# Attention and gated FFN on one core: norm roots in a PSUM bank, bias adds in the up stage, the even output's transposes in slot 15, scores for the maxima as pairs of 64-row tiles

## What is computed

```python
def attn(q, k, v, Wq, Wk, Wv, Wfc, bfc):          # q normalised, k = v = context
    score = einsum('bhqd,bhkd->bhqk', qh, kh) / sqrt(16)   # 32 heads of 16, K and V repeated 4 times
    out = einsum('bhqk,bhkd->bhqd', softmax(score), vh)
    return merge(out) @ Wfc.T + bfc
def ffn(x, w_gating, w_linear):                   # operands cast to fp8, results bf16
    return qdot(gelu(qdot(x, w_gating[0])) * qdot(x, w_gating[1]), w_linear)
x = x + attn(layernorm(x), ctx, ctx, ...)
x = x + ffn(layernorm(x), ...)
```

## Time and profile before

| | us |
|---|---|
| median of 3 runs | 466.82 |
| lowest and highest | 464.19, 467.55 |
| span of the profiled execution | 470.4 |
| busy: TensorE | 429.2 (91%) |
| busy: VectorE | 340.6 (72%) |
| busy: ScalarE | 314.8 (67%) |
| busy: GpSimd | 237.4 (50%) |
| `up` matmuls L640 (2048) | 130.0 |
| scores for the maxima L518 (128) | 57.3 |
| maxima L1060 (128) | 85.2 |

### The profile page before, as it was taken

One profiled execution on the slowest core, in us unless ns is written; L12 is line 12 of the kernel. 1 busy time (PEld: TensorE's weight loads), 2 busy tenths in 40 slices (PEclk: granted clock), 3 DMA queues, 4 the chain that ended last, 5 costly groups with the idle time before them and its releaser, 6 DMA issues.

```text
span 470.4 us, 11765 instructions
## 1 busy us (share of the span) xinstructions
PE 429.2 (91%) x4620; PEld 345.5 (73%) x4620; DVE 340.6 (72%) x689; ACT 314.8 (67%) x578; POOL 237.4 (50%) x226
## 2 busy tenths in 40 slices
PE   6867878979999799999999799999999799888997
PEld 6746756757887678877887678777887678547973
DVE  4775678957797778977787778877797778475442
ACT  6848875977479546977488646976488445875541
POOL 5677952896039611694049711793049510592000
PEclk9978889989999999999999999999999899999999
DMA  8797769253602460035402460045303151000001
GB/s 292 272 263 290 243 183 293 68 185 118 155 3 59 146 135 26 8 88 154 114 3 67 140 134 26 16 125 146 79 3 80 36 125 36 3 24 24 2 24 46
DMA packets 21239, 49.79 MB, mean 106 GB/s; under 512 B 4672, under 2 KB 5184, under 8 KB 21184
## 3 DMA queue, kind: packets, MB, share of 16 engines
q1 hardware_dynamic: 20862, 48.24, 35.8%
q10 hardware_dynamic: 322, 0.80, 0.7%
HBM read 23.86 MB, written 4.19 MB: 60 GB/s over the span
## 4 chain that ended last, share of the span: by engine, by line
PE 48%; POOL 19%; DVE 18%; ACT 5%; issue 5%; DMA 3%; ACTq 1%; POOLq 0%; SPq 0%; DVEq 0%
PE bank L640 18%; POOL plo L1264 13%; PE bank L660 6%; PE bank L441 5%; PE bank L518 5%; PE bank L442 4%; PE bank L443 4%; DVE mneg L1060 4%; DVE xn L1110 3%; POOL xr L1272 3%; PE bank L551 2%; DVE osum L1073 2%; PE bank L476 1%; DMA qs<-cq 1%; DVE bn L1013 1%
## 5 line engine op out<-in xcount | busy, mean ns | idle before, releaser
L1264 POOL TENSOR_TENSOR plo<-p,phi 128x512 f16<-128x512 f32 x128 | 152.5, 1213 | 56.7 <-ACT phi L836 56.4
L640 PE MATMUL bank<-x2T,wgate 128*128 128x128 fp8e4 x2048 | 130.0, 220 | 0.6 <-ACT x2T L848 0.5
L640 PEld LDWEIGHTS bank<-x2T,wgate 128*128 128x128 fp8e4 x2048 | 116.8, 98 | 14.0 <-issue 5.4
L1060 DVE TENSOR_REDUCE mneg<-bank 128x4 fp32r<-128x512 f32 x128 | 85.2, 687 | 21.0 <-PE bank L518 20.6
L833 ACT ACTIVATE p<-bank 128x512 f32<-128x512 f32 x128 | 77.7, 607 | 22.7 <-PE bank L551 20.3
L836 ACT ACTIVATE phi<-bank 128x512 f16<-128x512 f32 x128 | 77.5, 605 | 0.0
L660 PE MATMUL bank<-wlin,act 128*128 128x512 fp8e4 x256 | 73.4, 382 | 0.0
L859 ACT CAST ff<-bank 128x512 bf16<-128x512 f32 x64 | 37.5, 586 | 52.8 <-PE bank L640 52.7
L569 PEld LDWEIGHTS bank<-vt,plo 128*128 128x128 f16 x512 | 31.8, 97 | 41.9 <-issue 21.0
L551 PE MATMUL bank<-qs,ks 98*128 98x512 f32 x128 | 55.7, 435 | 6.1 <-ACT phi L836 2.9
L855 ACT ACTIVATE gate<-bank 128x512 bf16<-128x512 f32 x64 | 38.2, 597 | 32.2 <-PE bank L640 31.2
(11 more groups left out here) (113 smaller groups left out, 832.5 us busy)
## 6 DMA issues: line engine op xcount, KB each, us to landing
qs<-cq SPq DMA_DIRECT2D x90, 128.0 KB, 2.4
stage<-in_w SPq DMA_DIRECT2D x14, 512.0 KB, 5.5
ks<-khl SPq DMA_DIRECT2D x96, 64.0 KB, 2.0
cin<-in_ctx SPq DMA_DIRECT2D x8, 512.0 KB, 4.1
xr<-in_x SPq DMA_DIRECT2D x16, 256.0 KB, 4.4
out<-xr SPq DMA_DIRECT2D x16, 256.0 KB, 2.5
xr<-in_w SPq DMA_DIRECT2D x6, 512.0 KB, 5.7
raw_g<-in_w SPq DMA_DIRECT2D x4, 512.0 KB, 6.3
```

The source lines that it names most:

```text
L640: mm = pe.matmul(out[:, h * SEQ:(h + 1) * SEQ], wgate8[:, UH * v + h, kk, part, :], x2T[:, b % NB, kk, :], start=kk == 0, stop=kk == KT - 1)
L1060: dve.tensor_reduce(dst[:, :, 2 * half:2 * half + 2, j].rearrange("p a r -> p r a"), bank_of("S", q, i, s)[:, :].rearrange("p (r a k) -> p ...
L1264: pool.tensor_tensor(plo[:, e % PBUF, :], p32[:, e % P32BUF, :], phi[:, e % PBUF, :], ALU.subtract).then_inc(plo_ok, 1)
```

## The change

1. *Roots in PSUM.* The root of the first norm (two columns) and of the odd sequence's second norm (one column) is copied to three columns of bank G1 (`roots_1`, `roots_2`). `norm_apply_psum` and `norm2_apply_psum` read x from SBUF and the root, broadcast over 512 columns, from PSUM, in one `scalar_tensor_tensor` in place of a `tensor_scalar` with two SBUF columns. The even sequence's second norm and round 0 keep the old form. `project_out` of the odd sequence, which overwrites G1, waits for `xn_ok`.
2. *Bias.* Both `add_bias` of round q move from slots 5 and 8 of round q to the end of GpSimd's slots of round q - 1, behind the even root.
3. *Even output.* `turn_out`, `out_hi` and `out_lo` of the even sequence move from unit 0 to slots 15 and 16 and from bank T0 to G1.
4. *Scores.* A group is one (K = 64, N = 512) matmul on rows 0 to 63 and one on rows 64 to 127, to the two banks of a pair, with one semaphore and one maximum of 1024 columns. Groups 0 and 1 stand in slots 17 and 18, groups 2 to 7 in units 0 to 5. Group 1 takes the T pair, the others A.

```diff
-S_EARLY = {True: {16: 1, 17: 1, 18: 2}, False: {15: 1, 16: 1, 17: 1, 18: 2}}
+S_EARLY = {17: 1, 18: 1}
+M_EARLY = {18: 1}
+S_UNITS = {4: (2, 2, 1, 1), 8: (1, 1, 1, 1, 1, 1, 0, 0), 12: (0,) * 12}
+EVEN_TURN = 15
...
+                    for side in range(2):
+                        take_bank("S", q, i, j, side)
+                for side in range(2):
+                    rows = slice(64 * side, 64 * side + 64)
+                    mm = pe.matmul(bank_of("S", q, i, j, side)[:, :], cq[rows, 0, j, tok(i)],
+                                   kmask[rows, 2 * side:2 * side + 2, :, tok(i)], start=True, stop=True)
+                mm.then_inc(s_done, 1)
...
                     pe.wait_ge(aoT_lo, b + 1)
+                    if chain_in_e(b) and b and b + 5 <= BATCHES:
+                        pe.wait_ge(xn_ok, b + 5)
...
+                    if p and n == EVEN_TURN:
+                        turn_out(NB * p)
...
+            def roots_2(b):
+                dve.wait_ge(rstd2_ok, b + 1)
+                dve.tensor_copy(root(NB), rstd2[:, b % NB:b % NB + 1]).then_inc(root2_ok, 1)
...
+            def norm2_apply_psum(b):
+
+                i = b % NB
+                dve.wait_ge(root2_ok, (b + 1) // NB + 1)
+                if b >= NB:
+                    dve.wait_ge(x2T_done, b - 1)
+                dve.scalar_tensor_tensor(xn2[:, i, :], xr[:, b % RING, :], mv2[:, i, 0:1], root(NB).broadcast_to([P, D]),
+                                         ALU.subtract, ALU.mult, saturate=False).then_inc(xn2_ok, 1)
...
-                dve.tensor_reduce(dst[:, :, 2 * half:2 * half + 2, j].rearrange("p a r -> p r a"),
-                                  bank_of("S", q, i, s)[:, :].rearrange("p (r a k) -> p r a k", r=2, a=2),
+                dve.tensor_reduce(dst[:, :, :, j].rearrange("p a r -> p r a"),
+                                  group_banks(q, i, j)[:, :, :].rearrange("p h (r a k) -> p (h r) a k", r=2, a=2),
                                   AX_X, ALU.max, negate=True).then_inc(max_ok, 1)
...
-                    for i in range(NB):
-                        if p and n == BIAS_SLOT[i]:
-                            add_bias(p, i)
                     if n == chain["rstd"]:
                         norm2_rstd(c_b)
                 if p:
                     norm2_rstd(NB * p)
+                if q < NP:
+                    for i in range(NB):
+                        add_bias(q, i)
```

More of the change, by code:

```diff
@@ L1149, in _ @@
             queries_lo(0, 0)
-            for s in range(4):
-                maxima(0, 0, s)
+            for g in range(2):
+                maxima(0, 0, g)
             queries_lo(0, 1)
-            for s in range(4, SBANKS):
-                maxima(0, 0, s)
-            for s in range(SBANKS):
-                maxima(0, 1, s)
+            for g in range(2, SGROUPS):
+                maxima(0, 0, g)
+            for g in range(SGROUPS):
+                maxima(0, 1, g)
             late = list(W_DVE)
@@ L1165, in _ @@
                     if q < NP and n < SLOTS:
-                        for s in range(early, early + M_EARLY[first].get(n, 0)):
-                            maxima(q, 0, s)
-                        early += M_EARLY[first].get(n, 0)
+                        for g in range(early, early + M_EARLY.get(n, 0)):
+                            maxima(q, 0, g)
+                        early += M_EARLY.get(n, 0)
                     for at, b in downs:
@@ L1175, in _ @@
                         out_lo(c_b)
+                    if p and n == EVEN_TURN + 1:
+                        out_lo(NB * p)
                     if n == chain["residual"]:
@@ L1200, in _ @@
                 u0, c_b = UPB * up_batches(p)[0], NB * p
-                per = TILES // ups if q < NP else 0
                 for k in range(ups):
-                    if p and k == 0:
-                        out_lo(c_b)
                     if q < NP and k == 0:
-                        for s in range(early, sum(S_EARLY[first].values())):
-                            maxima(q, 0, s)
-                        early = sum(S_EARLY[first].values())
+                        for g in range(early, sum(S_EARLY.values())):
+                            maxima(q, 0, g)
+                        early = sum(S_EARLY.values())
                     if p and k == 2:
@@ L1212, in _ @@
                         out_lo(c_b + 1)
-                    for s in range(per * k, per * k + per):
-                        if s % per == per // 2 and k:
-                            product(u0 + k - 1)
-                            act_fp8(u0 + k - 1)
-                        if s >= early:
-                            maxima(q, *divmod(s, SBANKS))
-                    if not per and k:
+                    for g in range(early, early + S_UNITS[ups][k]):
+                        maxima(q, *divmod(g, SGROUPS))
+                    early += S_UNITS[ups][k]
+                    if k:
                         product(u0 + k - 1)
```

149 lines of the change are left out of this document (76 added, 73 removed).

## The result

The changed kernel takes 487.54 us (median of 4 executions, 485.59 to 490.27), beside 467.19 us for the kernel before (median of 4). The ratio is 1.043, 95% interval 1.037 to 1.049. 472 us had been forecast, with a range of 459 to 484: the sign was right, the size wrong, and the time lies outside the range. The profiled execution's span is 485.6 us against 470.4, so +15.2 us where the sum of terms had said +4.9.

A forecast was written before the change was run, and what follows sets the result against it. TensorE bounds odd rounds; in even rounds it waits on a norm held by GpSimd. Terms -7.8 - 1.5 - 2.5 - 1.2 + 15.0 + 3.2 - 0.3 = +4.9 us on a 470.4 span: span near 475, median near 472, range 459 to 484.

The forecast's parts named there:

- (a): Odd batch's second norm: with roots in PSUM, 0.6 to 0.7 us and no GpSimd wait; -7.8, clock -1.5 us.
- (b): Bias adds leaving the attention stage: -2.5 us in round 7, -1.2 in round 1, 0 in rounds 2 to 6.
- (b, c, d) round 1: Round 1: -1.2 us from moving the bias adds, +2.5 from the longer round with grouped scores.
- (c, d) an undisturbed round from 2 to 6: Each such round: +2.5 us from waits in the up stage, the 1.6 saved on scores already included.
- second add blocked: Even norm in the up stage passed over for a second GpSimd add: 1.25 us more, 3 of 7 times; +3.2 us.
- start and round 0: First 16 maxima in 8 instructions, -0.3 us; round 0's two 1.5 us waits offset by less score time, 0.
- (d): Up stage: groups wait for full maxima, residual and xn come later; +2.5 us a round, +15.0 over six rounds.
- (c): Scores in the up stage: a pair costs 0.28 to 0.30 us; -1.6 us a round of TensorE work.
- the upper bound of the same step: Pair of scores in the up stage: 0.85 us if nothing overlaps across the change of tile.
- The other bound: Pair of scores in the up stage: 0.57 us if its halves don't overlap.
- the pair costs more: Rival, up stage: a pair costs 0.57 us, giving 478 us, or 0.85, giving 484; chance 0.22.
- The rival: Clock falls after waits at x2 transposes and group 5, up to 1.5 us in six rounds, 481 us; chance 0.06.

The follow-up runs named there:

- roots_only: The kernel before with only the roots moved to PSUM (part 1 of the change); 463.4 us, ratio 0.995 to the kernel before.
- roots_bias_up: The kernel before with the roots in PSUM and the bias adds in the up stage (parts 1 and 2 of the change); 467.5 us, ratio 0.994.
- full_tile: The changed kernel with both matmuls of a score group on all 128 rows instead of 64; 487.1 us, ratio 1.044 to the kernel before.
- full_tile_again: The changed kernel with both score matmuls of a group on all 128 rows, run a second time; 485.2 us, ratio 1.042 to the kernel before.

## Why the prediction was wrong

By its own steps, on the profiled executions:

| step | forecast | measured |
|---|---|---|
| (a) roots | -9.3 | -9.8 (roots_only) |
| (b) bias, round 7 | -2.5 | -1.5 (-1.3 in roots_bias_up) |
| (b, c, d) round 1 | +1.3 | +1.0 |
| (c, d) an undisturbed round from 2 to 6 | +2.5 | +3.3 |
| second add blocked | +3.2 in all | 0 (never more than one) |
| clock in rounds 4 and 5 | 0 | +4.3 (2.7 and 1.6) |
| start and round 0 | -0.3 | +4.9 |

*Right.* (a): L1146 was given 0.6 to 0.7 us and takes 0.75, in all eight rounds, and the 2.6 us wait for ao is gone. The second half of the rule on the shared ports that the prediction took from the Trainium skill ("SBUF — State Buffer", section "Who interferes with whom"), for which no row stood before, now has one: with a single tensor read from SBUF the norm is never held back (747 to 749 ns). (d): the replay of round 3 named three of the four waits and came near their sum: forecast 1.1 before group 2, 2.2 at the transposes, 0.9 at group 5, 0.4 at unit 4, 4.6 us in all; measured 0.76 before group 0, which it had not named, and 0.40 before group 2, 1.92, 0.75, none, 3.8 us. xn took 1.47 us where 1.4 was said, a maximum steps by 1.14 where 1.15 was said.

*Wrong in size, (c).* "I take 0.28 to 0.30: independent rows, separate banks." A pair costs 0.51. I looked at the two halves, which do overlap, and not at what stands around them, although the upper bound of the same step had the change of tile in it. The other bound was off too: "0.57 if they don't" took two scores at 0.28 each, but the second of two in a row costs 0.23 (full_tile), so that 0.51 is also the price without any overlap. The "-1.6 us a round of TensorE work" did not come: 50.59 against 50.69 us. 50.7 - 1.6 + 4.6 would have been 53.7; it is 50.6 + 3.8 = 54.4. So the work was 1.5 us a round dearer than the sum had it, and the waits 0.8 shorter. That is the rival "the pair costs more" (478 us by its middle value), and five rounds of +0.8 are 4 us of the miss.

*Wrong, the term for the second add.* +3.2 us stood in the sum for a norm passed over a second time; it lasted 1.47 or 1.48 us in all six rounds. This hid the dear pair: rounds 2, 3 and 6 came out at +0.5, +3.3 and -1.0 us, where the sum had +0.4, +3.0 and -1.1. That agreement is luck, two errors that cancel.

*Wrong, (d), round 0.* "Round 0 has two groups in a unit (two waits of 1.5 us) but six scores' time less and a start of round 1 set by arriving data: 0." The waits are there (1.42 us, twice), but the start of round 1 isn't set by data alone: at half clock 16 `up` matmuls last 1.87 us in the rows instead of 1.07, and round 1 begins 4.9 us later. In full_tile and full_tile_again, which have the same two waits (1.41 us each) but 3.4 us at half clock there, it begins at 81.7 and 83.0 us, beside 82.0 before.

*Wrong, the clock.* The sum had nothing for it. The rival had it (up to 1.5 us in each round, 481), with a chance of 0.06, and only after the waits of the later rounds. In the profiled execution it costs 4.3 us there and about 4.9 in round 0: over 9 us, more than the pairs. Pairs 4.0, round 0 5.2, later clock 4.3 and round 7 1.0 make 14.5 us; the second add that never came (-3.2), the roots (-0.5) and round 1 (-0.3) leave 10.5, which is, but for rounding, the 10.3 us by which the sum for the span was missed (475.3 against 485.6). Why the clock stays down longer in this kernel remains open.

*The range* reached to 484 for a dearer pair alone. Dearer pair and clock came together, and the range treated them as alternatives.

## What to carry to other kernels

Price an instruction of another tile shape by the beat of the row around it, with one change there and one back: a matmul at half height between full ones cost almost twice the full-height one, and two full-height ones in a row cost less than twice one. Where work is taken off an engine and the freed time depends on another engine's order, look first at what now stands ahead of the critical step: two maxima of 1.2 us moved behind it gave back 1.2 us a round. And a GpSimd instruction moved into idle time can still hold back VectorE: of the two places tried for the bias adds, one slowed the norm and the other the product and its cast, and the round was 52.3 us with either.
